# Asking for x a block sooner in the projection stage, and letting GpSimd start earlier

## What is computed

```python
x = x + attention(layernorm(x))      # q, k, v: 256x256 projections; 16 heads; softmax over 2048; Wo
x = x + channel_mix(layernorm(x))    # token shift with mu_r, mu_k; sigmoid gate; relu squared; W_v
```

## Time and profile before

| | us |
|---|---|
| runs | 2822.83, 2825.59, 2824.67; median 2824.67 |
| profiled execution | 2828.22 |
| its span, first to last instruction | 2825.8 |
| PE busy | 2753.7 (97%) |
| DVE busy | 2496.2 (88%) |
| ACT busy | 2489.3 (88%) |
| POOL busy | 373.6 (13%) |
| mean granted PE clock | 0.993 |

### The profile page before, as it was taken

How to read it: one execution, slowest core, us unless ns; L and a number is a source line. 1 busy time by engine, 2 the same in 40 slices (tenths; PEclk the granted TensorE clock), 3 DMA queues, 4 the chain that set the end, 5 groups by cost and what they waited for, 6 DMA issues and landing times.

```text
span 2825.8 us, 60098 instructions
## 1 busy us (share of the span) xinstructions
PE 2753.7 (97%) x23676; PEld 934.3 (33%) x23676; DVE 2496.2 (88%) x4853; ACT 2489.3 (88%) x2863; POOL 373.6 (13%) x751
## 2 busy tenths in 40 slices
PE   9779999999999999999999999999999999999999
PEld 6434222222222222222222222222222222224776
DVE  4445999999999999999999999999999999985674
ACT  6546999999999999999999999999999999997555
POOL 6545000000000000000000000000000000113451
PEclk9889999999999999999999999999999999999999
DMA  5443101010101010101010100000000100112531
GB/s 172 150 132 131 28 9 31 11 33 11 33 11 32 11 33 11 33 11 32 11 31 13 28 16 22 20 20 20 21 22 22 44 22 22 51 45 73 165 129 45
DMA packets 135290, 124.36 MB, mean 44 GB/s; under 512 B 49888, under 2 KB 117344, under 8 KB 135008
## 3 DMA queue, kind: packets, MB, share of 16 engines
q1 hardware_dynamic: 135008, 120.52, 13.9%
HBM read 72.75 MB, written 47.19 MB: 42 GB/s over the span
## 4 chain that ended last, share of the span: by engine, by line
PE 75%; SPq 10%; ACT 4%; DMA 3%; DVE 3%; issue 2%; POOL 1%; ACTq 0%
PE psum L1358 32%; PE psum L1261 17%; PE psum L1317 15%; SPq L153 3%; PE psum L1789 2%; SPq L158 2%; PE psum L447 2%; PE psum L1276 2%; PE psum L1386 2%; SPq L126 2%; SPq L127 2%; DMA a_qs<-q_parts 2%; PE psum L1777 1%; ACT m_gate L957 1%; ACT p_x L957 1%
## 5 line engine op out<-in xcount | busy, mean ns | idle before, releaser
L1039 DVE TENSOR_REDUCE a_mx<-psum 128x1 f32<-128x512 f32 x3096 | 1946.3, 683 | 96.8 <-PE psum L1317 76.5
L1261 PE MATMUL psum<-a_qs,a_ks 50*128 50x512 f16 x4096 | 792.0, 383 | 10.0 <-ACT p_x L957 0.5
L1317 PE MATMUL psum<-a_ks,a_qs 48*128 48x512 f16 x3596 | 696.3, 384 | 43.5 <-DVE a_mx L1039 34.6
L957 ACT ACTIVATE m_gate<-psum 128x1024 f32<-128x1024 f32 x684 | 674.3, 1033 | 37.4 <-PE psum L1261 34.6
L957 ACT ACTIVATE p_x<-psum 128x1024 f32<-128x1024 f32 x682 | 672.4, 1033 | 38.1 <-PE psum L1261 35.4
L957 ACT ACTIVATE m_y<-psum 128x1024 f32<-128x1024 f32 x682 | 672.3, 1033 | 37.7 <-PE psum L1261 34.7
L1358 PE MATMUL psum<-m_gate,a_vst 128*32 128x256 f32 (+1 forms) x4568 | 413.5, 434 | 0.8
L1358 PE MATMUL psum<-m_y,a_vst 128*32 128x256 f32 (+1 forms) x4552 | 412.0, 433 | 0.8
L1358 PE MATMUL psum<-p_x,a_vst 128*32 128x256 f32 (+1 forms) x4568 | 412.0, 432 | 0.8
L1261 PEld LDWEIGHTS psum<-a_qs,a_ks 50*128 50x128 f16 x4096 | 198.7, 93 | 604.7 <-ACT m_gate L957 144.1
L1034 DVE CUSTOM_DVE_ANT_0 a_copied<-psum,a_copied 128x512 f32<-128x512 f32 x500 | 323.5, 684 | 22.8 <-PE psum L1317 22.7
(11 more groups left out here) (149 smaller groups left out, 1616.1 us busy)
## 6 DMA issues: line engine op xcount, KB each, us to landing
m_x<-x SPq DMA_DIRECT2D x24, 512.0 KB, 5.3
a_qs<-q_parts SPq DMA_DIRECT2D x384, 32.0 KB, 2.1
sums<-a_o SPq DMA_DIRECT2D x256, 34.0 KB
q_parts<-m_split SPq DMA_DIRECT2D x16, 512.0 KB, 3.1
v_rows<-m_v SPq DMA_DIRECT2D x16, 512.0 KB, 3.1
k_parts<-m_split SPq DMA_DIRECT2D x16, 512.0 KB, 3.9
a_ks<-k_parts SPq DMA_DIRECT2D x64, 128.0 KB
a_vin<-v_rows SPq DMA_DIRECT2D x64, 128.0 KB, 5.5
```

Of the source, the lines that this page charges most:

```text
L957: ac.activation(p_sb[n % WEIGHTS][:, 2 * pair:2 * pair + 2, :], psum[:, at:at + 2, :], ACT.Exp, scale=SCALE).then_inc(s_exp, 1)
L1039: dve.tensor_reduce(peak, psum[:, bank(at), :], AX.X, ALU.max).then_inc(s_mx, 1)
L1261: mm = te.matmul(psum[:, pair_of_banks(u) + par, :], ks[row:row + MR, (it // QB) % 2, pair, c * P:(c + 1) * P], qs[row:row + MR, it % QRIN ...
L1317: te.matmul(psum[:, bank(slot(n, par)), :], qs[row:row + SR, pit % QRING, at:at + P], keys, start=True, stop=True).then_inc(s_sp, 1)
```

## The change

SP asks for x(b+5), not x(b+4), at the head of block b, ahead of the stores of b; the load of x(4) stays where it was, ahead of the loop. Each load keeps the wait for the norm that frees its buffer. POOL's first low parts wait for the last `second` step (block 1's tokens) instead of the last `third` one. The fills of rows stand behind blocks 1, 2, 5 and 6 instead of 0, 1, 5 and 6; the buffers and halves that they fill are the same in the same order. PE begins with 16 waking matmuls, not 21.

```diff
-    WAKE, AWAKE = 21, 3
+    WAKE, AWAKE = 16, 3
...
+        def next_x(blk):
+
+            if blk + 4 >= BLOCKS:
+                return
+            if blk < 3:
+                alone.wait(sp, 0, ("norm1", f"second{TT - 1}", f"third{TT - 1}")[blk])
+            if blk not in (1, 2):
+                an.wait(sp, blk, f"norm{TT - 1}")
+            load(blk + 4)
...
+        next_x(0)
         for blk in range(BLOCKS):
-            if blk + 4 < BLOCKS:
-                if blk < 3:
-                    alone.wait(sp, 0, ("norm1", f"second{TT - 1}", f"third{TT - 1}")[blk])
-                if blk not in (1, 2):
-                    an.wait(sp, blk, f"norm{TT - 1}")
-                load(blk + 4)
+            next_x(blk + 1)
...
-        alone.wait(pool, 0, f"third{TT - 1}")
+        alone.wait(pool, 0, f"second{TT - 1}")
         for blk in range(BLOCKS):
             lesser_parts(blk, blk % 2)
-            if blk < 2 or 5 <= blk < 7:
+            if blk in (1, 2, 5, 6):
                 least.wait(pool, blk, f"part1_kd{KH - 1}")
-                inputs.set_unit(pool, int(blk >= 2), (blk + 1) % 2 if blk >= 5 else blk)
+                inputs.set_unit(pool, int(blk >= 5), (blk - 1) % 4 % 2)
```

## The result

The changed kernel took 2774.4 us, the median of 6 runs (2772.7 to 2775.68), against 2825.25 for the kernel before (6 runs, 2822.83 to 2827.23): ratio 0.982, 95% interval 0.9807 to 0.9833. The profiled execution took 2775.0, its span 2773.2. The profiled execution of the kernel before lies 3.0 us above its median, this one 0.6, so gains read from block starts come out 1.5 to 3 us larger than gains of medians.

What follows compares the result with a forecast made beforehand. PE was taken as the bound, idle mainly in the projection stage behind late loads of x. Terms -1.1 - 6.7 - 44.1 + 0.5 = -51.4 took the profiled 2828.2 to 2776.8; median 3.5 lower, 2773 us, range 2769 to 2786.

Steps and rivals of the forecast that it cites:

- The load a block sooner: Blocks 6 to 11: x arrives in time, leaving only PE's own work, 82.1 us instead of 126.2; gain 44.1 us.
- The spare time: Even blocks, from first q projection T_b: x lands T_b+8.3, statistics want it T_b+11.7 (3.4 us spare), PE asks T_b+15.6.
- GpSimd's start and the fills: Blocks 0 to 5: GpSimd's earlier low parts and moved fills let them run at PE's 11.5 us; gain 6.7 us.
- The price of sharing with VectorE: VectorE's second pair beside GpSimd: small operations +2.2 us, four large ones 0 to +4.5; cost 0 to 0.8, taken 0.
- The worst end of 0.8: Block 2's tokens ready only at 34.5, PE asking at 33.3: 0.8 us said to be lost.
- The Trainium skill's rule: VectorE instructions with two SBUF inputs or two-port mode block behind GpSimd instructions reading SBUF; by it 0.8 us lost.
- The start: Before the first projection: five fewer waking matmuls remove 10 fast records; gain 1.1 us.
- The fear of a slower clock behind 16: At the start: if the clock rose later, the 24 records behind the waking matmuls ran slow; loss of 1.5 us.
- The stores of block 4: SP's queue at blocks 4 and 5: these stores land up to 1 us late for ACT in block 6; cost 0.5.
- wait for late stores: Rival: loads of x ahead of the stores delay their landing, and ACT waits; 2783 us, chance 0.07.
- none of PE for VectorE in blocks 6 to 12: Rival: VectorE becomes the bound in odd blocks, 3.4 us lost in each of three; 2784 us, chance 0.05.
- SP's wait for the norm: Rival: this wait, now ahead of block b's stores, delays them past ACT's slack; slower, 2836 us, chance 0.03.

Runs made afterwards that it cites:

- e1: The kernel before with only the loads of x a block sooner; GpSimd's start, the fills and 21 waking matmuls as before: 2780.8 us.
- e5: The changed kernel with each load of x(b+5) moved behind the store of q of block b: 2775.1 us.
- e6: The changed kernel with each load of x(b+5) moved behind the store of v of block b: 2806.5 us.
- e2: The kernel before with only GpSimd's earlier start and the moved fills; loads of x and 21 waking matmuls as before: 2818.1 us.
- e4: The changed kernel with the fills behind blocks 0, 1, 5 and 6 again: 2778.0 us.
- e8: The changed kernel with 10 waking matmuls instead of 16: 2776.7 us.
- e3: The changed kernel with GpSimd's first low parts waiting for the third block's tokens again: 2781.9 us.

## Why the prediction was right

It said 2773 (2769 to 2786) and 2776.8 for the profiled execution; measured were 2774.4 and 2775.0. The gain of 51.4 was measured as 50.9 between the medians and 53.2 between the profiled executions. That the median would lie 3.5 us under the profile was carried over from the kernel before and did not hold (0.6): most of the two misses, 1.4 up for the median and 1.8 down for the profiled execution, is this, and the closeness of each is partly luck. By its own steps:

- *The load a block sooner*: predicted 82.1 us for blocks 6 to 11, measured 163.63 - 81.74 = 81.9; gain 44.3 against 44.1. In e1, with the loads alone, the same blocks gain 42.6 and block 5 another 4.5. e5 and e6 show the mechanism from the other side: a request 5 to 6 us later costs nothing, one 13 us later 32 us in all. The spare time was put at T_b+11.7 for the statistics and T_b+15.6 for PE. e5 shows where it ends in block 6: x landed at T_6+13.8 and cost 0.1 us, since PE's next pack, at T_6+15.0, has 1.4 us of VectorE's work before it. The transfer was faster (4.9) than the 6.0 taken from the one chain row.
- *GpSimd's start and the fills*: predicted 69.0 for blocks 0 to 5, measured 68.7; gain 7.0 against 6.7, and 6.8 in e2 alone. The step was right in sum, but its reason was not whole. 4.5 of these microseconds are block 5's, which e1 shows the loads give back by themselves; what GpSimd adds to the loads is 4.3, and 1.7 of that lies in block 6, as ACT waits there for late stores without it. And I let the moved fills count only as work of GpSimd. e4 shows that at their old place they would have held VectorE through 3.5 us and cost 2.4 us of PE. The price of sharing with VectorE was put at 2.2 us for the small steps and 0 to 4.5 for the four large ones; here the small ones took 5.3 us (23.81 to 29.14), 2.7 more than alone, and the four large ones 3.86, 2.5 more. Block 2's last tokens were ready at 33.0, between the 30.0 and 34.5 of the text; PE asked for the first ones at 33.31 and waited for none: cost 0, as taken. The worst end of 0.8 does not follow from the numbers beside it, 34.5 less 33.3 being 1.2.
- *The Trainium skill's rule* (SBUF — State Buffer, "Who interferes with whom") is that a two-port VectorE instruction fully blocks behind GpSimd. The trace agrees, and e4 shows the part that had no row before, that a GpSimd instruction which only writes does it too (7.21 us against 1.38). The prediction had tied the rule to GpSimd instructions that read SBUF, and the expectation of e4, 1.4 us beside the fill, failed on that.
- *The start*: predicted 1.1, measured 1.13 between the two profiled executions; over nine executions 0.9, with a scatter as large. The fear of a slower clock behind 16 was not borne out (squares 1.92 us). With 10 the clock was low (e8), but because it fell after a pause, not because it rose later.
- *The stores of block 4*: predicted 0.5 lost, nothing was (this 0.5 was in the sum, but not in the T_12 of 164.0: 216.04 less 51.4 is 164.6). They were out at 78.0, 1.4 us earlier than I had worked out, since the second head's rows of k could go out at 70.7, not 72. e3 shows that this was near: 7.4 us later on the queue, and ACT waits 3.77.
- *Rivals*: no wait for late stores, none of PE for VectorE in blocks 6 to 12. SP's wait for the norm, now ahead of the stores, showed once, without cost: x(6) could be asked for only at 33.02, when block 2's tokens were ready, and q of block 1 was stored at 33.44, 2.1 us after its low part was there (31.36). The stores behind it wait for later parts anyway. In block 6 q was stored at 90.19, when its low part was there.

## What to carry to other kernels

When a load waits behind stores on one queue, read where its data is wanted and where its buffer comes free; if the buffer is free earlier, ask for it ahead of the stores. Beyond the spare time each microsecond is paid again in every second block, and the wait brings a lower clock with it: 6 us later cost nothing, 13 us later 32. When an engine is let go earlier, look at which instructions of the two then stand side by side (here GpSimd's and VectorE's, e4), and move a long fill away from the other's work that is waited for.

## What the hardware showed that I had not expected

A GpSimd fill of 32x4096 float16 (3.50 us), which has no input, held a VectorE `tensor_scalar` on 128x256 float32 for its whole length (3.65 us, e4): four of them took 7.21 us instead of 1.38. Beside low parts (1.16 us each) they took 3.86.

The waking matmuls reach the higher speed at a time that changes from execution to execution: the same 32 records took 6.54, 6.33, 5.67, 5.95 and 5.50 us, the same 42 took 7.90, 7.79, 7.09 and 7.14. PE runs 6 or 7 of them in a microsecond until about 8 us in the kernel before and the changed one, until about 6 in e4 and e6, and 9 to 12 afterwards, while the granted clock reads 1.00 throughout. So a gain of one microsecond in the start of this kernel can be read only over several executions.
